# VectorE scans ahead of weighing in the first eight steps of three images

## The reference: what is computed

```python
# token mixing
scores   = einsum('btd,bsd->bts', q, k)
retained = einsum('bts,bsd->btd', d_gamma * scores, v)
h = where(y >= 0, y, prelu_a * y)              # y = retained @ Wo + bo
# selective scan, INNER = 128 channels, 16 states
x_conv = silu(x_main @ W_conv + b_conv);  dt = softplus(x_conv @ W_dt + b_dt)
h_new  = exp(dt[..., None] * A) * h + dt[..., None] * B_t * x_t    # along 1024 tokens
y_t    = (h_new * C_t).sum(states) * silu(x_gate)
h = layernorm(h + y @ W_out + b_out)
# routed feed-forward: two layers, one of 16 experts for each 64 tokens
h = layernorm(h + ffn(h))
```

## Time and profile before

| | us |
|---|---|
| median of 3 runs | 341.44 |
| lowest and highest of them | 341.2, 349.24 |
| the profiled execution | 342.13 |
| its span, first to last instruction | 339.7 |
| VectorE busy | 262.1 |
| GpSimd busy | 259.4 |
| TensorE busy (matmuls) | 282.3 |
| ScalarE busy | 190.8 |
| mean granted TensorE clock | 0.934 |

### The profile page before, as it was taken

The page is one execution under the profiler, slowest core; times in us unless marked ns, Lnnn a source line. Parts: engine busy times, 40 slices in busy tenths (PEclk is TensorE's granted clock), DMA queues, the critical chain, the costliest instruction groups (busy, mean ns, idle before and its releaser), DMA issues. The chain is left out here.

```text
span 339.7 us, 4780 instructions
## 1 busy us (share of the span) xinstructions
PE 282.3 (83%) x1478; PEld 162.2 (48%) x1478; DVE 262.1 (77%) x287; ACT 190.8 (56%) x298; POOL 259.4 (76%) x136
## 2 busy tenths in 40 slices
PE   8898839875678689989797799997855999779996
PEld 5423412433336233356473243565644579458764
DVE  2565678998778988998898899987998799269420
ACT  3004831336895451679946525789377686657322
POOL 1028057999899989998998979989999999949300
PEclk9999957999698799999999799997898999979999
DMA  7970495686689997766799977668999999767000
GB/s 244 415 283 0 145 307 223 215 267 234 244 275 327 309 319 301 268 227 243 263 323 327 312 274 291 205 248 275 296 311 344 346 359 373 268 170 243 21 0 15
DMA packets 47128, 85.88 MB, mean 253 GB/s; under 512 B 7936, under 2 KB 24832, under 8 KB 46848
## 3 DMA queue, kind: packets, MB, share of 16 engines
q1 hardware_dynamic: 46704, 84.43, 73.9%
q10 hardware_dynamic: 400, 1.17, 1.1%
HBM read 75.62 MB, written 1.57 MB: 227 GB/s over the span
## 5 line engine op out<-in xcount | busy, mean ns | idle before, releaser
L1212 POOL TENSOR_TENSOR hc<-h,c_row 128x1024 f32<-128x1024 f32 (+1 forms) x79 | 154.6, 1967 | 22.4 <-DVE h L1341 19.4
L1201 POOL TENSOR_TENSOR ub<-u,b_row 128x1024 f32<-128x1024 f32 (+1 forms) x49 | 98.2, 2004 | 13.0 <-DVE u L1387 11.3
L925 ACT ACTIVATE decay<-delta,neg_a 128x512 f32<-128x512 f32 (+1 forms) x64 | 51.2, 811 | 62.6 <-DVE h L1341 62.2
L664 PEld LDWEIGHTS acc_y<-pack,hc 128*128 128x128 f32 x512 | 61.3, 147 | 39.3 <-issue 23.9
L664 PE MATMUL acc_y<-pack,hc 128*128 128x128 f32 x512 | 74.6, 286 | 3.1 <-POOL hc L1212 3.1
L1341 DVE TENSOR_TENSOR_SCAN h<-decay,ub 128x512 f32<-128x512 f32 (+1 forms) x41 | 66.0, 1610 | 14.4 <-ACT decay L925 7.3
L606 PE MATMUL work<-q,kT 64*128 64x512 f32 x112 | 36.0, 722 | 16.8 <-DVE mixed L1367 12.5
L1367 DVE TENSOR_TENSOR mixed<-gam,work 128x512 f32<-128x512 f32 x56 | 35.5, 676 | 7.2 <-PE work L606 6.6
L952 ACT ACTIVATE decay<-u 128x512 f32<-128x512 f32 (+1 forms) x42 | 26.4, 639 | 21.5 <-DVE h L1341 21.3
L617 PE MATMUL acc_r<-mixed,v_sb 128*64 128x512 f32 x128 | 37.0, 659 | 1.1 <-DVE mixed L1367 1.0
L1341 DVE TENSOR_TENSOR_SCAN h<-decay_own,decay 128x512 f32<-128x512 f32 (+1 forms) x23 | 34.5, 1498 | 1.1
(11 more groups left out here) (210 smaller groups left out, 357.9 us busy)
## 6 DMA issues: line engine op xcount, KB each, us to landing
b_row<-bc_dram SPq DMA_DIRECT2D x64, 512.0 KB, 5.1
c_row<-bc_dram SPq DMA_DIRECT2D x64, 512.0 KB, 5.8
group_w<-expert_w SPq DMA_DIRECT2D x48, 128.0 KB, 4.7
gam<-gammaT SPq DMA_DIRECT2D x8, 512.0 KB, 10.1
expert_w<-routed_w SPq DMA_DIRECT2D x1, 2048.0 KB, 17.9
gam<-expert_w SPq DMA_DIRECT2D x16, 128.0 KB, 5.3
x_in<-xT SPq DMA_DIRECT2D x4, 256.0 KB, 9.0
pack<-packed ACTq DMA_DIRECT2D x1, 788.0 KB, 6.5
```

Of the source, the lines that this page charges most:

```text
L664: mm = nc.tensor.matmul(acc_y[:, to:to + P], hc[:, at:at + P], ident, start=(job.state == 0 and c % 4 == 0), stop=(job.state == STATES - 1 ...
L925: op = nc.scalar.activation(target, delta[:, job.image % 2, columns], ACT.Exp, scale=neg_a[:, job.state:job.state + 1])
L1201: nc.gpsimd.tensor_tensor(ub[:, ring(made, job.halves)], u[:, job.image % 2, tokens(q)], b_row[:, ring(job.at, job.halves)], ALU.mult).the ...
L1212: nc.gpsimd.tensor_tensor(hc[:, here], h[:, here], c_row[:, here], ALU.mult).then_inc(hc_ready, job.halves)
```

## The change: what it does

In phases 0, 1 and 2, in steps 0 to 7, VectorE's instruction for the scan of step k now stands ahead of the two that weigh block n of the head's scores; in phase -1 (no scan) nothing moves. No instruction is added or taken away, and no other engine's stream is touched.

```diff
@@ the loop of VectorE's stream
                     if k == 0:
                         scan_job(0)
-                    if head is not None and n < TILES:
+                    if p == -1 and n < TILES:
                         weight_scores(head, n)
                     if p == -1 and n == 1:
                         folded_weights()
...
                                 last_part(b, m)
                             if 2 * n + i in HALF_DVE:
                                 half_tail(0, HALF_DVE[2 * n + i])
+                    if p >= 0 and head is not None and n < TILES:
+                        weight_scores(head, n)
                     if head is not None and n == 8:
                         prelu(head)
```

## The result

The changed kernel takes 358.85 us (median of 4 runs, 357.82 to 360.92) against 341.68 for the kernel before in the same comparison (4 runs): ratio 1.0473, 95% interval 1.0436 to 1.051. That is slower, as forecast, and 5.9 us above the forecast 353.

A forecast was written before the change was run, and what follows sets the result against it. Bound: the loop of VectorE's scan and ScalarE's decays, 3.70 us per state, with GpSimd's chain beside it. Terms -1.4 + 6.0 + 6.0 + 1.1 = 11.7 us gave 353.8 profiled, 353.1 median, forecast 353; range 346.5 to 360.5.

The forecast's parts named there:

- the chain through ScalarE: Last part, phases 1 and 2: ScalarE waits for TensorE's late results, delaying decays and scans; 6.0 us per phase, chance 0.60.
- Spread over the moved weighings: Main rival of the follow-up experiments, not of the prediction: the loss lies in the new order itself; no chance given.
- 20 to 24: Stretch from the scan of state 4 to that of state 8 in phase 1; forecast 6.0 us longer.
- The chain's second link: Step 6, phases 1 and 2: ScalarE's Relu waits for TensorE, making state 8 late by 1.8 us beyond earlier delays.
- Scan 6: Phases 1 and 2: scan of state 6 starts 2.8 us later, behind ScalarE's wait for the output product.
- State 8 in phase 1: Its multiplication starts 5.9 us late, from 2.8, 1.3 for weighing 7 and 1.8 of ScalarE lateness; taken as 6.0.
- the Square waits by about 3 us: Sign in the profile after: ScalarE's Square (line 1046) waits about 3 us for TensorE's output product, phases 1 and 2.
- Phase 0: No image in its last part: scan 3 comes 2.7 us earlier, the eighth weighing costs 1.3; gain 1.4 us.
- The boundary to phase 1: Change of image where no weighing lies between images any longer; taken as 0, between -0.4 and +0.3 us.
- The boundary to phase 2: Change of image: TensorE starts late at the low clock, ScalarE's copy delays the decays of state 3; 1.1 us more.
- The falling clock: Rival: TensorE's clock falls inside phases 1 and 2 after idle gaps; 3 to 6 us more, about 357.5, chance 0.21.
- 40 to 48: Stretch from the scan of state 8 in phase 2 to scan 0 of phase 3; forecast change 0.

## Why the prediction was right, and where it was too low

- **What bounds, and the chain through ScalarE: right, and shown from both sides.** Loosening the chain takes the loss away with VectorE's order kept (1.0023), and making the chain late brings the loss of this link with VectorE's order left alone (1.0119). "Spread over the moved weighings" is out by the marks: with all weighings moved and the chain loosened, 20 to 24 costs 1.2 and no more. The two halves of the steps, 1.0124 and 1.0346, agree, but prove less, since their intervals touch the rival's and each half has a seam at step 4 that costs something of its own. The chain's second link, the Relu ahead of state 8's decays, was made shorter only together with the other edits.
- **Scan 6: 2.8 forecast, 2.8 measured** (idle 3.04 against 0.24). **State 8 in phase 1: 6.0 forecast, 5.92 measured**, with 1.26 of weighing and 1.90 of wait, where the sum had 1.3 and 1.8. The sign "the Square waits by about 3 us" was a slip: the forecast's own rows give 141.5 less 137.3, 4.2 us, and 4.24 was measured.
- **Phase 0: 1.4 forecast, 1.88 in the trace, 1.5 and 1.4 in the two where it stands alone, nothing clear of noise in the time.** GpSimd took over at scan 3, as written, for 2.7; the weighing took back 1.2.
- **The boundary to phase 1: 0 forecast, 1.40 measured.** The step that failed is "I take 0, between -0.4 and +0.3": the forecast works out the gain, and not the loss. Its own steps for phase 2, without the 0.6 of turned rows, put scan 3 at an estimated 13.75 us after scan 0, where it stood at 13.20: 0.55 more. The other 0.85 are the low clock, which held the retention at 1.97 (for 1.6) and the transposes at 1.61 (for 1.1). The 1.73 us that this scan had waited for GpSimd's `ub` before didn't cover it. The boundary to phase 2 came at 1.13 for 1.1. With the transposes ahead of the scores both are gone.
- **The falling clock: the rival came true once, at its own price.** The 2.1 us gap in step 6 was foreseen, 2.09 measured, in both phases. In both the scores after it took 1.13; in phase 2 the clock fell behind them, and the retention and the transposes took 1.92 and 1.88 for 1.08 and 1.09. The wait of line 1070 grew by 1.63, for a price of 1.6 that the forecast had worked out from other pieces, the scores and the retention. The sum that was forecast took none. The Trainium skill, "TensorE: Matmul & The Clock Gate", section "HAM oscillation — how this bites in real kernels", describes such falls for waits that are longer than this one, so by it no gap of 2.09 us would have lowered the clock. Here six such gaps were traced, in step 6 of both phases of this kernel, of the one with phases 1 and 2 alone and of the one with steps 4 to 7; two of them did (phase 2 of the first two).
- **40 to 48: 0 forecast, 1.15 measured.** ScalarE brought the first half of u for phase 3 late (VectorE waited 1.31 us at 266.72), behind its reads of the layer norm, after TensorE had run steps 14 and 15 of phase 2 at the low level:

```profile
254.00:258.00 4.00, 3.53 (x17) 3.45 (x18) 3.86 (x4) 1.39 (x3) 3.50 (x3) 0.50 0.98 298
```

  The kernel before has such a stretch ahead of phase 3 too, from 234 to 240, and it ends 11 us before that scan; here it lasts from 249 to 263 and ends 4 us before it. That the new order makes it longer was not shown. The 33.27 of the kernel before is also at the low end: seven of the nine other traces have 33.6 to 33.9.
- **The start: 0.92 us ahead of scan 0**, where the change moves nothing. Scan 0 began between 46.28 and 47.20 in all traces, and at 46.98 in the kernel with the old order and the late output product. It is not the change's.

So the four terms that were forecast as -1.4, 6.0, 6.0 and 1.1 came to -1.9, 5.9, 5.9 and 1.1, 11.1 (unrounded) instead of 11.7. What the sum left out is the boundary to phase 1 (1.4), the fall of the clock (1.6), the last two stretches (0.7) and the start (0.9), 4.6 together. The medians are 17.2 apart where these two executions' spans are 15.7 apart; the rest is the difference between one execution and another. That 358.85 lies within the forecast's range is in part luck: its upper end was made of falls of the clock inside an image, 3 to 6 us, which gave 1.6; the other 3.0 of the 4.6 are terms that it had at nothing.

No kernel here beats the one before beyond its interval. The changed order in phase 0 alone is the best of them, at 0.9973 and 0.9993.

## What to carry to other kernels

- Two orders in which A and B alternate look alike on their own engine; what differs is which of them a third engine has seen when it starts. Follow the moved instruction's semaphore through the streams of all engines, in their written order, until it comes back to the one that was moved: here VectorE, TensorE, ScalarE, VectorE.
- An engine with plenty of idle time (ScalarE, busy 56%) can still be on the path. It is where a wait stands in its stream ahead of work that others need at once that counts; a repair is to move the read behind that work, or what it reads ahead of the wait. The second was run alone and took 3.04 us of idle time to 0.24; the first only together with it.
- At the ends of a row of alternating steps count one by one which gap an instruction leaves and which it enters: at the boundary to phase 1 the weighing left a gap of 0.7 us and entered a place without any:

```profile
113.08 1.23 DVE L1313 TENSOR_TENSOR decay<-decay,b_row 128x1024 f32<-128x1024 f32 x1 [0.72 <-ACT decay L952]
```

## What the runs showed of the hardware that was not expected

- The same gap of 2.09 us in TensorE's work, after the same eight or so us of dense matmuls, left the clock at the 2.4 GHz level in phase 1 (1.13 us for the four matmuls after it, 1.08 for the next four) and was followed by 1.2 GHz in phase 2 (1.13, then 1.92).
- In steps 12 to 15 of phase 1 a gap of 1.1 us stands ahead of the experts' matmuls (line 723 or its like). Behind it they ran at the high level in three kernels (the changed one, phases 1 and 2 alone, steps 4 to 7) and at the low one in three others (output product early, transposes first, steps 0 to 3). Here one that held, gap of 1.12, and one that fell, gap of 1.10:

```profile
176.71 0.39 PE L718 MATMUL tail<-onehot,bias_w 96*128 96x512 bf16 x1 [1.12 <-DVE f L1402]
176.94 1.90 PE L723 MATMUL tail<-f,group_w 128*128 128x64 f32 x16
```

```profile
172.88 0.39 PE L718 MATMUL tail<-onehot,bias_w 96*128 96x512 bf16 x1 [1.10 <-DVE f L1406]
173.11 3.18 PE L723 MATMUL tail<-f,group_w 128*128 128x64 f32 x16
```

  So the length of the gap alone doesn't tell whether the clock falls. In the kernel with the transposes ahead of the scores it then stayed at 0.50 for some 10 us although TensorE was busy in all of the windows 176 to 184.
- In step 6 of phase 2 the fall cost as much on the path (1.63 us) as its matmuls lost (0.84 and 0.79); with one in steps 12 to 15, 24 to 32 went from 35.36 to 39.54 us. The runs of the kernel with the transposes first lie between 348.47 and 353.49 us; that falls of the clock make this spread is likely and not shown.
